# Query products on two row halves of the array in layer 0 of a two-layer graph network

## What is computed

```
Q, K, V = x @ WQ, x @ WK, x @ WV          # (12500, 128) each
Eh      = edge_attr @ WE                  # (212500, 128)
score   = K[src] * Q[dst] / sqrt(16) * Eh # per head of 16
score   = exp(clip(score.sum(-1), -5, 5))
wV      = segment_sum(V[src] * score, dst)
Z       = segment_sum(score, dst)
h       = x + wV / (Z + 1e-6)             # then batch norm
```

## Time and profile before

| | |
|---|---|
| median of three runs | 5763.41 us (5759.13 to 5770.78) |
| span of the profiled execution, first to last instruction | 4693.0 us |
| median less span | 1070.4 us |
| layer 0's gathers, first to last | 81.05 to 2286.13 us |
| busy over the span | PE 3812.3, PEld 3161.6, DVE 3158.1, ACT 1078.1, POOL 3369.7 us |
| mean granted TensorE clock | 0.670 of 2.4 GHz |

### The profile page before, as it was taken

One profiled execution on the slowest core, in us unless ns is written; L12 is line 12 of the kernel. 1 busy time (PEld: TensorE's weight loads), 2 busy tenths in 40 slices (PEclk: granted clock), 3 DMA queues, 4 the chain that ended last, 5 costly groups with the idle time before them and its releaser, 6 DMA issues. The chain is left out here.

```text
span 4693.0 us, 76906 instructions
## 1 busy us (share of the span) xinstructions
PE 3812.3 (81%) x19332; PEld 3161.6 (67%) x19333; DVE 3158.1 (67%) x8279; ACT 1078.1 (23%) x4010; POOL 3369.7 (72%) x3437
## 2 busy tenths in 40 slices
PE   6889899989989988888898977777777777777778
PEld 5777777777778877767567755655555556555555
DVE  1877677677777776777646866666666666666657
ACT  3100010000000000000034433333333333333324
POOL 3677777777777777777557777777777777777752
PEclk9887787787776787888687555555555555555559
DMA  7666665666666666666424322222222222222224
GB/s 279 182 182 184 176 189 176 179 183 181 183 181 182 182 183 174 185 179 183 148 86 97 61 61 61 61 61 61 61 61 61 61 61 60 60 61 61 61 58 154
DMA packets 376029, 593.47 MB, mean 126 GB/s; under 512 B 151298, under 2 KB 204520, under 8 KB 374488
## 3 DMA queue, kind: packets, MB, share of 16 engines
q0 software_dynamic: 132880, 330.18, 27.4%
q1 hardware_dynamic: 241544, 255.24, 18.2%
q10 hardware_dynamic: 1552, 7.43, 0.4%
HBM read 551.16 MB, written 40.54 MB: 126 GB/s over the span
## 5 line engine op out<-in xcount | busy, mean ns | idle before, releaser
L393 POOL DMA_INDIRECT kv_g<-kv_table,idx x1661 | 1678.2, 1010 | 568.0 <-issue 498.7
L1065 POOL DMA_INDIRECT xg<-xl_table,idx x1661 | 1583.0, 953 | 519.3 <-issue 498.6
L1130 PEld LDWEIGHTS ps_sum<-pw,xg 128*128 128x128 f32 x3328 | 740.9, 328 | 165.9 <-DVE pws L1271 165.5
L1130 PE MATMUL ps_sum<-pw,xg 128*128 128x64 f32 x3328 | 819.1, 428 | 4.7 <-DVE pws L1271 2.2
L452 PE MATMUL ps_sum<-kv_g,hot 128*64 128x136 f32 x3328 | 606.6, 339 | 246.8 <-issue 245.8
L1117 PE MATMUL ps_tops<-ident,top 128*64 128x128 f32 x832 | 285.9, 447 | 518.7 <-DVE top L1243 518.4
L452 PEld LDWEIGHTS ps_sum<-kv_g,hot 128*64 128x64 f32 x3328 | 480.9, 167 | 314.9 <-issue 310.2
L438 PE MATMUL ps_pair<-w,eat 128*128 128x128 f32 x3328 | 616.3, 342 | 5.1 <-issue 5.1
L438 PEld LDWEIGHTS ps_pair<-w,eat 128*128 128x128 f32 x3328 | 524.2, 240 | 109.3 <-issue 71.7
L442 PE MATMUL ps_pair<-qw,hott 64*128 64x128 f32 x3328 | 583.9, 326 | 2.9 <-DMA qw<-q_table 2.9
L1229 DVE SCALAR_TENSOR_TENSOR ps_lg<-raw 128x256 f32<-128x256 f32 x416 | 185.3, 445 | 573.4 <-ACT raw L1178 566.7
(11 more groups left out here) (160 smaller groups left out, 4684.9 us busy)
## 6 DMA issues: line engine op xcount, KB each, us to landing
eat<-in_edges SPq DMA_DIRECT2D x416, 256.0 KB
local<-local_table SPq DMA_DIRECT2D x416, 128.0 KB, 3.8
kv_g<-kv_table,idx POOLq DMA_INDIRECT x1661
xg<-xl_table,idx POOLq DMA_INDIRECT x1661
qw<-q_table SPq DMA_DIRECT2D x416, 32.0 KB
adw<-ad_row SPq DMA_DIRECT2D x416, 32.0 KB, 5.1
kv_table<-kv_out SPq DMA_DIRECT2D x25, 512.0 KB, 2.6
xl_table<-xl SPq DMA_DIRECT2D x25, 264.0 KB, 2.8
```

Source lines behind the costliest of these rows:

```text
L393: nc.gpsimd.indirect_dma_start(out=kv[:, u, k, 0:2 * D], out_offset=None, in_=m["kv_table"], in_offset=bass.IndirectOffsetOnAxis(ap=idx[:, ...
L1065: nc.gpsimd.indirect_dma_start(out=xg[:, u, k], out_offset=None, in_=m["xl_table"], in_offset=bass.IndirectOffsetOnAxis(ap=idx[:, u // B, ...
L1130: nc.tensor.matmul(ps_sum[:, b, 0:W], xg[:, u, k, 0:D], pw[:, b, k], start=(k == 0), stop=(k == K - 1))
```

## The change

The array of TensorE has 128 rows, and the query products use 64 of them. Now blocks 0 and 1 of a chunk stand on partitions 0 to 63 and blocks 2 and 3 on partitions 64 to 127: `hott` and `local` are 128 partitions by 256 instead of 64 by 512, and the 64 query rows are loaded twice, once into each half. The four query matmuls alternate between the halves (k = 0, 2, 1, 3). For that the PSUM buffer is laid out anew: of each chunk's two banks, bank h holds the gate products of blocks 2h and 2h + 1 in its first half and their query products in its second, so that matmuls of different row halves write different banks. `line` becomes the partition's number modulo 64.

```diff
@@ edges0
-        qw = sb("qw", [W, 4, D])
-        local = sb("local", [W, 4, CE])
-        line = sb("line", [P, 1])
+        qw = sb("qw", [P, 4, D])
+        local = sb("local", [P, 4, CE // 2])
+        line, fold = sb("line", [P, 1]), sb("fold", [P, 1])
-        hott = sb("hott", [W, 2, CE])
+        hott = sb("hott", [P, 2, CE // 2])
-        ps_eh = ps_pair[:, 0].rearrange("p b (k d) -> p b k d", d=D)
-        ps_q = ps_pair[:, 1].rearrange("p b (k d) -> p b k d", d=D)
+        ps_eh, ps_q = ps_pair[:, :, :, 0:CE // 2], ps_pair[:, :, :, CE // 2:CE]
@@ load_window, load_local
-                sp.dma_start(qw[:, u % 4], m["q_table"][bass.ds(base, W), :]).then_inc(window_in[u % 4], 16)
+                for half in range(2):
+                    sp.dma_start(qw[at(half, W), u % 4], m["q_table"][bass.ds(base, W), :]).then_inc(window_in[u % 4], 16)
-                sp.dma_start(local[:, u % 4], m["local_table"][bass.ds(c, 1), :].partition_broadcast(W)).then_inc(local_in[u % 4], 16)
+                for half in range(2):
+                    sp.dma_start(local[at(half, W), u % 4], m["local_table"][bass.ds(c, 1), at(half, CE // 2)]
+                                 .partition_broadcast(W)).then_inc(local_in[u % 4], 16)
@@ spread_out
-                    nc.tensor.matmul(ps_eh[:, b, k], eat[:, u % 4, at(k, P)], m["w"][:, WE], start=True, stop=True)
-                pe.wait_ge(window_in[u % 4], landed(c, u % 4, 16, 4))
+                    nc.tensor.matmul(ps_eh[:, b, k // 2, at(k % 2, D)], eat[:, u % 4, at(k, P)], m["w"][:, WE], start=True, stop=True)
+                pe.wait_ge(window_in[u % 4], landed(c, u % 4, 32, 4))
                 pe.wait_ge(hott_ready, c + 1)
-                for k in range(K):
-                    mm = nc.tensor.matmul(ps_q[:, b, k], hott[:, b, at(k, P)], qw[:, u % 4], start=True, stop=True)
+                for j in range(K // 2):
+                    for half in range(2):
+                        mm = nc.tensor.matmul(ps_q[:, b, half, at(j, D)], hott[at(half, W), b, at(j, P)], qw[at(half, W), u % 4],
+                                              start=True, stop=True)
@@ vector, once, before the walk
+            do(nc.vector.tensor_scalar(fold[:], line[:], W - 0.5, float(W), ALU.is_gt, ALU.mult))
+            nc.vector.tensor_tensor(line[:], line[:], fold[:], ALU.subtract).then_inc(line_split, 1)
@@ one_hot_turned
-                dve.wait_ge(local_in[u % 4], landed(c, u % 4, 16, 4))
-                nc.vector.tensor_scalar(hott[:, u % 2], local[:, u % 4], line[0:W], None, ALU.is_equal).then_inc(hott_ready, 1)
+                dve.wait_ge(local_in[u % 4], landed(c, u % 4, 32, 4))
+                nc.vector.tensor_scalar(hott[:, u % 2], local[:, u % 4], line[:], None, ALU.is_equal).then_inc(hott_ready, 1)
@@ attend
-                nc.vector.tensor_tensor(prod[:].rearrange("p (k d) -> p k d", d=D), ps_q[:, b],
-                                        kv[:, u, :, 0:D], ALU.mult).then_inc(mult, 1)
+                nc.vector.tensor_tensor(prod[:].rearrange("p (h k d) -> p h k d", h=2, d=D),
+                                        ps_q[:, b].rearrange("p h (k d) -> p h k d", d=D),
+                                        kv[:, u, :, 0:D].rearrange("p (h k) d -> p h k d", h=2), ALU.mult).then_inc(mult, 1)
-                nc.vector.tensor_tensor(prod[:], prod[:], flat(ps_eh[:, b]), ALU.mult).then_inc(gated, 1)
+                halved = prod[:].rearrange("p (h e) -> p h e", h=2)
+                nc.vector.tensor_tensor(halved, halved, ps_eh[:, b], ALU.mult).then_inc(gated, 1)
```

More of the change, by code:

```diff
@@ L280, in edges0 @@
         gated, scored = sem("gated"), sem("scored")
+        line_split = sem("line_split")
         weighed, valued, summed, added = sem("weighed"), sem("valued"), sem("summed"), sem("added")
@@ L559, in attend @@
                 short = 16 * (K - -(-LAST // P)) if isinstance(c, int) and c == NC - 1 else 0
-                flat = lambda v: v.rearrange("p k d -> p (k d)")
                 dve.wait_ge(turned, c + 1)
                 dve.wait_ge(kv_in[u], landed(c, u, 16 * K, U) - short)
-                nc.vector.tensor_tensor(prod[:].rearrange("p (k d) -> p k d", d=D), ps_q[:, b],
-                                        kv[:, u, :, 0:D], ALU.mult).then_inc(mult, 1)
+                nc.vector.tensor_tensor(prod[:].rearrange("p (h k d) -> p h k d", h=2, d=D),
+                                        ps_q[:, b].rearrange("p h (k d) -> p h k d", d=D),
+                                        kv[:, u, :, 0:D].rearrange("p (h k) d -> p h k d", h=2), ALU.mult).then_inc(mult, 1)
                 dve.wait_ge(mult, c * 2 + 1)
-                nc.vector.tensor_tensor(prod[:], prod[:], flat(ps_eh[:, b]), ALU.mult).then_inc(gated, 1)
+                halved = prod[:].rearrange("p (h e) -> p h e", h=2)
+                nc.vector.tensor_tensor(halved, halved, ps_eh[:, b], ALU.mult).then_inc(gated, 1)
                 dve.wait_ge(gated, c + 1 + LEAD)
@@ L590, in _ @@
                 one_hot(c, c)
+            dve.wait_ge(line_split, 1)
             one_hot_turned(0, 0)
```

## The result

The changed kernel takes 5785.41 us (5782.93 to 5793.34) against 5759.13 (5749.99 to 5770.78) for the kernel before: a ratio of **1.005** (95% interval 1.0037 to 1.0064), slower, where I had forecast 5748 and faster.

What follows compares the result with a forecast made beforehand. The prediction took POOL's queue to bound layer 0. Terms -29 + 12 - 4 + 2 = -19 us, taken as -15, gave a 4678 us span and 5748 us median, 0.3% faster; range 5705 to 5825.

Steps and rivals of the forecast that it cites:

- I make the sum against the span and carry the difference to the median unchanged: Whole kernel: terms summed on the 4693.0 us span; the 1070.4 us up to the median, without rows, kept unchanged.
- rival 4: Layer 0: more is won, by free phases (up to -107 us) or PE-bound unseen time (208 to 349 us); chance 0.07.
- POOL's queue sets layer 0's end: Layer 0's walk: POOL's gathers and issues fill 2177 of 2205 us; PE, 90% busy, only follows.
- The loads: SP's five transfers per chunk instead of three: hidden by loading three chunks ahead, except +2 us at the start.
- my other three terms: Layer 0: shorter comparison -29 us, new rhythm +12 us, query products -4 us.
- The query products: PE, layer 0: full overlap of row halves saves 0.84 us (1.2 GHz) or 0.50 (2.4) per chunk; only -4 us counts.
- Line 562: DVE's comparison, line 555 before: at 128 x 256 it takes 0.32 us, 0.15 us less.
- 191 x 0.15 = -29: Layer 0: 191 gathers held by the DVE each end 0.15 us earlier through the shorter comparison, -29 us.
- The new rhythm: Layer 0: 70 of 136 cheap fast chunks move to kinds where POOL loses 0.30 instead of 0.13 us, +12 us.
- Rival 2: Layer 0: POOL and DVE lock at a bad phase, +57 us, 5820 (range 5775 to 5850); chance 0.18.
- rival 3: PE stays at 1.2 GHz in layer 0, every chunk 5.80 us, +208 us at worst (5971); chance 0.08.

Runs made afterwards that it cites:

- e3_loads_doubled: Kernel before with the change's loads alone (query rows loaded twice, second copy unused; local places in two transfers), matmuls as before: 5809.5 us, 1.0095.
- e2_compare_twice: Changed kernel with the one-hot comparison made twice, first into a spare tile: 5680.4 us, where the changed kernel takes 5682.8.
- e3_compare_twice: Changed kernel with the one-hot comparison made twice, on a chip where the changed kernel takes 5793.1 us: 5780.5 us.
- e1_before_again: Kernel before, unedited, run again for a second trace: 4696.1 us, span 4694.1.
- e3_products_apart: Changed kernel with each query product placed behind one gate product, so that two row halves never stand next to each other: 6192.7 us, 1.0744.
- e1_three_dmas: Changed kernel with one transfer for both halves of the query rows and one for both halves of the local places: 5289.1 us, 1.1249.

## Why the prediction was wrong

**The step that failed** is the first: "I make the sum against the span and carry the difference to the median unchanged". The 1070 us were stalls inside layer 0 (6.4 to 6.6 us a chunk, not 5.2) and layer 1 (from the first to the last gather 2556 us on C, 2597 on A, 2095 on B), which the trace at hand didn't have. I had the right question as a part of rival 4 and took the opposite sign from it. PE isn't the bound in them: on A POOL waits 67 us for it and starts late by 528 us that no event explains.

**"POOL's queue sets layer 0's end."** Right on B. On A and C POOL is idle for 550 to 650 us beyond its issues, against 70 on B, most of it late starts; gathers and issues alone don't set the end there. What the change saves in gathers (1695.4 to 1641.9 on C) and in waits for PE (99 to 54) comes back as late starts (384 to 492), and PE's 340 us less of busy time on C brings nothing either. Why the late starts grow when the work shrinks isn't shown.

**The loads**, forecast as hidden, +2 us. On B they cost 9 us (2 to 17). On A they cost 51 us, shown by e3_loads_doubled, and this is more than the whole loss of 26 to 34. This is the term that turned the sign there. The rest of the change, by subtraction -16, comes near the -21 of my other three terms (-29, +12, -4), by luck: on B, where they can be seen, none of the three came out, as follows. How two loads cost 51 us isn't shown: no trace of the kernel before exists on A to set beside theirs, and whether SP's issues or the transfers do it stays undecided, as the experiments on that ran on B. C, where the change costs nothing, is unexplained too.

**The query products.** Full overlap was near the truth: 0.45 us less at 2.4 GHz (0.50 forecast), 0.66 at 1.2 GHz (0.84). The -4 us for POOL's waits didn't come on B, where they are 24 us for 19.

**Line 562** (555 before). 0.346 us for 0.32. But "191 x 0.15 = -29" misread what decides. e2_compare_twice and e3_compare_twice add 0.35 us of the same instruction and the gathers take 20 to 24 us *less*. Of the 201 long gathers (over 1.2 us) of the prediction 52 start in the comparison and 149 in line 576; in the changed kernel on B all 144 start in 576's successor, line 584, and none in 562. So the kind of hold that runs through the comparison is gone and the other is as frequent as before; I had both last 0.15 us less. That the DVE bars POOL is as the earlier trace rows show; what it costs depends on when the DVE comes to these lines and can't be had by scaling one of the durations.

**The new rhythm**, forecast as +12 us, was the term with the wrong sign on B. I counted chunks by how fast they were. The count was near: 70 chunks under 4.2 us from one first product to the next, where e1_before_again's trace has 124. But I held the loss of each kind fixed. 19 chunks take over 6.25 us where 111 did, and POOL's loss (gathers less 1661 x 0.946) is 48 / 416 = 0.12 us per chunk where it was 104 / 416 = 0.25; it fell in the chunks of every kind. The DVE now waits for gathers in most chunks and so starts in a fixed distance to them. On B the change gives -62.6 us, of which the gathers are -55.7 (1675.4 in e1_before_again to 1619.7); I had -15 for layer 0, a quarter of it. That the fixed distance is a good one I conclude from these counts; no run set it on purpose. Whether the shorter products or the shorter comparison make the new rhythm isn't separated either: e3_products_apart and e3_compare_twice were meant for that and ran on A.

**The rivals.** Rival 2 (lock at a bad phase) and rival 3 (the clock stays low) did not come: the gathers' sum fell on B and C, and the clock of the stretch is 0.85 for 0.76 on B, 0.76 for 0.69 on C. (In rival 2's sum 0.75 less 0.26 is 0.49 and not 0.45, which makes +93 of +86.) The slowdown on A came from the loads, which I had priced at +2. That 5785 lies inside my range is no merit of it: the range was drawn for other causes.

## What to carry to other kernels

Check that the trace's span and the timed median belong together before making any sum; a fifth of the time without a row meant here that the trace was of another condition than the timing. An engine whose queue is full beyond "busy" (POOL on B, 77% busy plus 0.30 us between gathers) is the bound, and a saving on PE reached it here only through the phases in which the engines meet. Where row halves are used, keep matmuls of one contraction height together (e3_products_apart), and don't save an issue by a transfer whose outermost dimension is 2 (e1_three_dmas).

## What the hardware showed that I had not expected

- One program takes 4699, 5686 or 5759 us on different chips. The longer times come with late starts about every 13 us: up to 8 us on ACT (median 3), up to 3 us on POOL, others on DVE and SP close to them, in traces whose instruction durations are otherwise the same (median of a gather 946 ns on B, 949 on A). What holds them up no row shows.
- Two matmuls of 64 rows on different halves overlap to 0.55 of their time at 2.4 GHz and 0.60 at 1.2, also when the halves follow in turn (0, 0, 1, 1): two records start 7 or 13 ns apart.
- A step between 128 and 64 rows of contraction leaves 0.22 us empty at 1.2 GHz and 0.12 at 2.4.
- A gather that starts while the DVE is in line 576, with two SBUF inputs, ends 0.82 us after that instruction: 1.36 for 0.95 us. A comparison added from SBUF to SBUF (e2_compare_twice) doesn't lengthen the gathers.
